# A cross-attention and mixture-of-experts kernel: filler matrix products on TensorE, another order of loads, logits one step later, one normalisation on VectorE

## The reference, cut to what matters

```python
def _L0_xattn_ref(q, k, v, igate_kernel, igate_bias, fgate_kernel, fgate_bias, outnorm_scale):
    x = concatenate([q, k, v], axis=-1)
    ig, fg = x @ igate_kernel + igate_bias, x @ fgate_kernel + fgate_bias
    # per head: log_D = (cs - cs^T, lower triangle) + ig^T, cs = cumsum(log_sigmoid(fg))
    # D = exp(log_D - max), C = (q k^T / sqrt(64)) * D
    # h = C / (max(|sum C|, exp(-max)) + 1e-6) @ v; then normalised per head, times scale
def _L0_ffn_ref(x, router_w, w1, w2):
    logits = einsum('nc,ec->ne', xf, router_w)          # 8 experts, two chosen
    h = gelu(einsum('nc,ech->enh', xf, w1)); y = einsum('enh,ehc->enc', h, w2)
    out = einsum('ne,enc->nc', comb, y)
x = x + _L0_xattn_ref(_layernorm(x), ctx, ctx, ...)     # x: (32, 128, 256) float32
x = x + _L0_ffn_ref(_layernorm(x), router_w, w1, w2)
```

## Time and profile before

| what | value |
|---|---|
| median of 3 runs (lowest to highest) | 759.17 us (758.35 to 761.41) |
| the profiled execution's own time | 766.17 us |
| its span | 764.3 us |
| TensorE busy in the span | 631.3 us (83%) |
| VectorE / ScalarE / GpSimd busy | 393.1 / 315.4 / 245.1 us |
| mean granted TensorE clock | 0.835 of 2.4 GHz |

### The profile page before, as it was taken

One profiled execution on the slowest core, in us unless ns is written; L12 is line 12 of the kernel. 1 busy time (PEld: TensorE's weight loads), 2 busy tenths in 40 slices (PEclk: granted clock), 3 DMA queues, 4 the chain that ended last, 5 costly groups with the idle time before them and its releaser, 6 DMA issues.

```text
span 764.3 us, 18354 instructions
## 1 busy us (share of the span) xinstructions
PE 631.3 (83%) x5879; PEld 504.2 (66%) x5879; DVE 393.1 (51%) x1094; ACT 315.4 (41%) x614; POOL 245.1 (32%) x192
## 2 busy tenths in 40 slices
PE   0684968779898994307999999999999999999991
PEld 0554756566877864206877777777777777777780
DVE  1452746667584555503555555555555555555550
ACT  1451562626444322102444444444444444444440
POOL 1101221626466266710222313233133231331322
PEclk9999856565565555557999999999999999999996
DMA  9878438294462122392385493943947639458321
GB/s 316 284 258 322 155 149 302 92 323 157 142 239 94 35 84 84 112 338 84 51 286 137 87 332 48 307 112 56 310 109 212 208 53 320 100 114 306 56 37 21
DMA packets 58964, 130.52 MB, mean 171 GB/s; under 512 B 6384, under 2 KB 38384, under 8 KB 57904
## 3 DMA queue, kind: packets, MB, share of 16 engines
q1 hardware_dynamic: 44384, 110.91, 40.8%
q0 software_dynamic: 13392, 18.10, 13.3%
q10 hardware_dynamic: 1152, 1.07, 0.4%
HBM read 188.49 MB, written 40.13 MB: 299 GB/s over the span
## 4 chain that ended last, share of the span: by engine, by line
PE 67%; DMA 12%; issue 6%; ACT 5%; DVE 4%; SPq 3%; POOL 2%; ACTq 1%; POOLq 0%; DVEq 0%
PE bank L661 15%; PE bank L647 9%; PE bank L649 9%; PE bank L648 8%; PE bank L663 8%; DMA xa<-in_x 7%; PE bank L540 4%; PE bank L565 3%; PE bank L483 3%; PE bank L525 2%; PE bank L510 2%; DMA out<-ct,dst 2%; PE bank L631 2%; POOL rows L1288 1%; DMA xrow<-rows 1%
## 5 line engine op out<-in xcount | busy, mean ns | idle before, releaser
L647 PE MATMUL bank<-dt,wring 128*128 128x128 f16 x1136 | 199.6, 220 | 2.4 <-ACT ct L824 1.2
L649 PE MATMUL bank<-dt,wring 128*128 128x128 f16 x1136 | 199.7, 220 | 0.0
L648 PE MATMUL bank<-dt,wring 128*128 128x128 f16 x1136 | 199.7, 220 | 0.0
L661 PE MATMUL bank<-wring,ct 128*128 128x512 f16 x568 | 192.5, 379 | 0.9 <-DVE ct L1222 0.7
L822 ACT ACTIVATE dt<-bank 128x512 f32<-128x512 f32 x142 | 84.9, 598 | 217.5 <-PE bank L649 211.0
L1222 DVE TENSOR_TENSOR ct<-dt,ct 128x512 f16<-128x512 f32 x142 | 98.4, 693 | 140.8 <-PE bank L663 99.2
L663 PE MATMUL bank<-wring,ct 128*128 128x256 f16 x568 | 154.8, 273 | 0.0
L1324 POOL DMA_INDIRECT out<-ct,dst x48 | 76.0, 1583 | 216.8 <-DMA out<-ct,dst 92.3
L647 PEld LDWEIGHTS bank<-dt,wring 128*128 128x128 f16 x1136 | 111.7, 98 | 27.0 <-issue 14.3
L648 PEld LDWEIGHTS bank<-dt,wring 128*128 128x128 f16 x1136 | 111.8, 98 | 0.9
L649 PEld LDWEIGHTS bank<-dt,wring 128*128 128x128 f16 x1136 | 111.9, 98 | 0.0
(11 more groups left out here) (140 smaller groups left out, 852.3 us busy)
## 6 DMA issues: line engine op xcount, KB each, us to landing
wring<-wsplit SPq DMA_DIRECT2D x284, 512.0 KB
wring<-in_w SPq DMA_DIRECT2D x16, 1024.0 KB, 11.4
xrow<-rows SPq DMA_DIRECT2D x71, 130.0 KB
wsplit<-wring SPq DMA_DIRECT2D x4, 2048.0 KB, 8.4
wsplit<-wcv SPq DMA_DIRECT2D x4, 2048.0 KB, 7.7
xa<-in_x SPq DMA_DIRECT2D x8, 512.0 KB, 10.7
kT<-in_ctx_t SPq DMA_DIRECT2D x8, 512.0 KB, 10.1
ctn<-in_ctx SPq DMA_DIRECT2D x8, 512.0 KB, 10.1
```

Source lines behind the costliest of these rows:

```text
L647: pe.matmul(o, hi, xT[k][:, c, :], start=(c == 0), stop=False)
L648: pe.matmul(o, hi, xT[k][:, CK + c, :], start=False, stop=False)
L649: mm = pe.matmul(o, lo, xT[k][:, c, :], start=False, stop=(c == CK - 1))
L661: pe.matmul(YP[k][:, 0:2 * D], gh[a][:, m4, :], wring[:, k, w:w + 2 * D], start=(a == 0 and m4 == 0), stop=False, skip_group_check=True)
```

## The change

- TensorE: a helper `dense` issues bfloat16 products of the identity with part of the mask into parts of accumulation banks whose contents nobody reads. Three of 256 columns follow each of the first three sequences of `gates`, two of 248 columns stand ahead of each `values`, and one of 256 columns follows each of the first three sequences of `logits`.
- TensorE: `logits` moves from the end of its step (for group m) to the next step (for group l), between `turn(n,0)` and `scores(t,0)`.
- SyncE: in a step the loads come first, and x is loaded one group further ahead (k + 1); then the weights that were split in the step before are stored, then the x1 of two steps back. At the start the loads of the first experts' weights come behind the constants and behind the keys and context of group 1.
- `SPLIT` gives each of the steps -1 to 6 one expert.
- The normalisation of x1 is done on VectorE, in the place of `x1_shift`, by one operation with two per-row scalars; ScalarE's `x1_norm` and the vector nm2 are gone.
- VectorE: the first operations of the router's chain come after `head_norm`.

```diff
-SPLIT = {-2: (0,), -1: (1, 2), 0: (3,), 1: (4,), 2: (5,), 3: (6,), 4: (7,)}
+SPLIT = {e - 1: (e,) for e in range(NE)}
...
             load_k(0)
+            sp.dma_start(gate_b[:, :, :], gate_b_in).then_inc(s_cst, 16)
             load_c(0)
-            sp.dma_start(gate_b[:, :, :], gate_b_in).then_inc(s_cst, 16)
             load_x(1)
-            load_w(0)
             sp.dma_start(cbf[:, :], cb.bitcast(BF16)).then_inc(s_cbf, 16)
...
             sp.dma_start(rwT[:, :, :], rw_t).then_inc(s_cst, 16)
+            load_k(1)
+            load_c(1)
+            load_w(0)
+            load_x(2)
...
-                if k is not None and k > 0:
-                    if k > 1:
-                        load_x(k)
+
+                if k is not None and k > 1:
                     load_k(k)
                     load_c(k)
-                for e in SPLIT.get(T, ()):
+                    if k + 1 < NG:
+                        load_x(k + 1)
+                for e in SPLIT.get(T - 1, ()):
                     store_w(e)
                     if e + 2 < NE:
                         load_w(e + 2)
-                if m is not None:
-                    store_x1(m)
+                if l is not None:
+                    store_x1(l)
...
+            def dense(o, count):
+
+                for _ in range(count):
+                    pe.matmul(o, cbf[:, B_IDENT:B_IDENT + P], cbf[:, B_MASK:B_MASK + o.shape[1]],
+                              start=True, stop=True, skip_group_check=True)
...
+                    if b < G - 1:
+                        dense(SB[:, 256:512], 3)
                 mm.then_inc(s_gt, 1)
...
+                dense(VB[b][:, 264:512], 2)
                 for h4 in range(NH):
...
+                    if b < G - 1:
+                        dense(SB[:, 256:512], 1)
                 mm.then_inc(s_lg, 1)
...
                 if n is not None:
                     turn(n, 0)
+                if l is not None:
+                    logits(l)
...
                     router_turn(m, 1)
-                    logits(m)
...
-                if m is not None:
-                    x1_norm(m)
...
-            def x1_shift(g):
+            def x1_norm(g):
                 dve.wait_ge(s_rs2, g + 1)
-                after(dve, s_xn2, 2 * g)
-                dve.scalar_tensor_tensor(nm2[:, :], mv2[:, :, 0], -1.0, rs2[:, :], ALU.mult, ALU.mult
-                                         ).then_inc(s_nm2, 1)
+                after(dve, s_sc[g % 2], 16 * (2 * G * (g // 2) + 1))
+                for b in range(G):
+                    ins = dve.tensor_scalar(rowb[g % 2][:, b, 0:D], xa[:, G * g + b, :], mv2[:, b, 0:1],
+                                            rs2[:, b:b + 1], ALU.subtract, ALU.mult)
+                    if b % 2 == 1:
+                        ins.then_inc(s_xn2, 1)
```

More of the change, by code:

```diff
@@ L159, in build @@
         rs2 = sb("rs2", [P, G])
-        nm2 = sb("nm2", [P, G])
         rT = sb("rT", [P, G, CK, P])
@@ L280, in build @@
         s_rs2 = sem("x1_rstd")
-        s_nm2 = sem("x1_shift")
         s_xn2 = sem("x1_normed")
@@ L458, in _ @@
             pe.wait_ge(s_gws, 1)
+            pe.wait_ge(s_cbf, 16)
+            def dense(o, count):
+                for _ in range(count):
+                    pe.matmul(o, cbf[:, B_IDENT:B_IDENT + P], cbf[:, B_MASK:B_MASK + o.shape[1]],
+                              start=True, stop=True, skip_group_check=True)
             def turn(g, h):
@@ L581, in step @@
                 if t is not None:
-                    if t == 0:
-                        pe.wait_ge(s_cbf, 16)
                     logd(t, 0)
@@ L747, in weights_high @@
                                ).then_inc(s_wh2, 1)
[L749 to L756, removed]
             def router_turned(g, h):
@@ L1090, in if_l @@
                         f(l, *a)
+                if_m(head_norm)
                 if_l(router, 0)
-                if_m(head_norm)
+                if_m(head_gamma)
                 if_l(router, 1)
-                if_m(head_gamma)
-                if_l(router, 2)
                 if t is not None:
                     scores(t, 0, 0)
+                if_l(router, 2)
+                if_m(residual)
                 if_l(router, 3)
-                if_m(residual)
                 if_l(router, 4)
@@ L1138, in step @@
                 if_l(slots)
-                if_m(x1_shift)
+                if_m(x1_norm)
                 if n is not None:
@@ L1263, in x1_rstd @@
                 after(pool, s_xn2, 2 * g)
-                after(pool, s_nm2, g)
                 pool.tensor_tensor(rs2[:, :], ve2[:, :], mhalf[:, 0:G], ALU.pow).then_inc(s_rs2, 1)
```

## The result

The change takes **737.84 us** (median of 4 runs, 732.68 to 741.41), beside 758.76 us for the kernel before on the same chip: a ratio of 0.972 (0.965 to 0.979). The forecast was 721 us in a range of 703 to 750: the sign and the range held, but 17 of the 38 us that were forecast are missing. The profiled execution took 736.62 us with a span of 734.8 us and a mean clock of 0.843.

The account below looks back on a forecast made before the run. Late x (steps 0 to 3) and TensorE, mostly at the lower clock level, bound the first part. Start 29.6, steps 28, 27.8, 145 and 24 make 254.4 against 293.3 us; draining +1; 38 off 759.2 gives 721 us, range 703 to 750.

Parts of the forecast that it names:

- the start: Before step 0: two megabytes of weights no longer ahead of x, gaining 6.6 us, so step 0 begins at 29.6 us.
- the loads: SyncE issues x a whole step earlier: -10.1 us in step 0, -4.9 us in each of steps 1 to 3.
- the clock's term: Full steps: fillers and moved logits raise TensorE's time at the upper clock level to 9.2 us, giving a 29.0 us step.
- F: TensorE's time at the upper clock level in a step; about 5 us before, forecast 9.2 us for a full step.
- plus 0.6 idle: TensorE in a full step: only 0.6 us idle added to 37.6 us of work at the lower clock level.
- the logits' wait: TensorE ahead of the logits: its wait for ScalarE goes when they move, -2.4 us in a full step.
- the router's chain on VectorE: Would start later with the moved logits; VectorE reaches it about in time, cost nothing; without that cover, up to 4 us.
- the x1 norm: On VectorE: four operations a step, 1.2 us in all, upper end 3.3; off the path unless VectorE is the bound.
- step 0, 1 and 7: Forecast lengths: step 0 28.0 us, step 1 27.8 us, step 7 24 us to the end of its head statistics.
- the draining: After the head statistics: draining gains six fillers, +1 us.
- the fillers pay where F grows: TensorE's full step: 20 fillers cost 4.8 us at the lower clock level and pay only if upper-level time grows.
- The rival of fillers without effect: Upper-level clock time stays 5 us, full steps take 33.2 us, gain 7.5 us: 752 us; chance 0.20.

Follow-up runs that it names:

- no_fill: The whole change with its filler products taken out; 728.04 us, 0.955 of the kernel before.
- loads_only: The kernel before with only SyncE's new load order and one expert for each step; 733.91 us, 0.963 of the kernel before.
- copy_first: The whole change with VectorE's copy of the logits ahead of head_norm, as before; 730.07 us, 0.956 of the kernel before.
- norm_scalar: The whole change with the x1 normalisation back on ScalarE, as before; 731.41 us, 0.961 of the kernel before.

## Why the prediction was right, and where it was wrong

**Right: the start and the loads, though not their size.** The start was forecast at 29.6 us and came at 29.9 (28.3 in no_fill), and no load of x is waited for in the steps. loads_only shows this term by itself, with the table of experts: 26 us. It was the only one that the gain needed. But what the prediction priced for it comes to 34.9 us: 6.6 at the start, 13.6 in step 0, and 4.9 in each of steps 1 to 3. Of the 9.8 us for steps 2 and 3 the trace of loads_only shows 0.6: the idle time went, and the clock was lower in the work that took its place.

**Right: the size of the clock's term, on the average.** I took F = 9.2 us at the upper level for a full step. From the windows the five steps have 10.3, 17.2, 10.4, 10.3 and 0 us: a mean of 9.6. TensorE's work of a full step was forecast at 37.6 us at the lower level; busy time plus F gives 38.0. What a mean hides is the scatter: step 6 stayed at 0.50 throughout and took 35.6 us, step 3 had 0.81 and took 27.7. The same kernel had 0.65 in one trace and 0.69 in another over steps 2 to 6. That the size came out is in part luck: the fillers brought only 2.1 to 4.4 us of it, and without them it was already 7.3 us a step, not the 5 that the sum started from.

**Wrong: "plus 0.6 idle".** This is the step that failed. I took the logits' wait off (2.4 us a step) and let nothing come for it; measured idle is 14.2 us in five steps, 2.8 each, as much as in steps 4 and 5 before (2.8 and 3.0 us; 0.6 in step 6, by the earlier trace rows). The missing 2.2 us a step is the whole difference between 29.0 and 31.2. The prediction did ask what would be late next, but it asked only for the router's chain on VectorE ("cost nothing; without that cover, up to 4 us"), and not who on TensorE waits for that chain's first operation: the gates, through the shared bank. copy_first shows that this wait, up to 1.4 us each time, is one of the causes. Nor did it ask what stands behind the x1 norm on VectorE: it priced the norm right (1.2 us forecast, 1.30 from its start to the scan's) and called it off the path, while the maximum's turn waits for the very next operation, for 4.5 us in five waits (0.6 in norm_scalar).

**Wrong: step 0, 1 and 7.** Step 0 took 19.6 us in this trace instead of 28.0. By its rows it ran at the lower level at first (the first `logd`'s products, 1.01 us at 29.89) and at the upper from 36.9 us on (the second's, 0.62 us), although the clock's column, which does not tell the levels apart this early, reads 1.00. In the second trace it took 26.75 us, so this is luck of the trace and not a gain that was missed. Steps 1 and 7 were 3.8 and 3.4 us over: in step 1 TensorE idles for 4.0 us of 31.6 (in the second trace for 0.9 of 28.7), in step 7 for 5.4 of 27.4. Step 7's term had no wait in it, and there is one of 4.5 us ahead of its second scores. By the rows it hangs on the last expert's low halves, which the new table lets run into this step, and on GpSimd's powers; loads_only has 2.3 us of it, and no run takes the two apart. Together with 11.2 us in steps 2 to 6 and 0.3 at the start this is the 10.3 us by which the head statistics came later than forecast; the draining gave 2 back.

**Wrong: that the fillers pay where F grows.** The prediction said so and took the growth as enough. Its own numbers held the break-even: 4.8 us a step go in, so F must grow from 5 to 9.8, and the F of 9.2 lay under that. The same sum without fillers, 32.8 + 0.6 - 5, is 28.4 us, less than the 29.0 with them; I never wrote it down. no_fill bears it out: 0.955 against 0.972 and 0.970, and 30.5 us as the mean of its steps 2 to 6 against 31.2 and 30.9. The rival of fillers without effect is refuted by the clock and by its 752 us; what holds of it is that the fillers gained nothing. As to the rule of the Trainium skill (TensorE: Matmul & The Clock Gate, Part 4) that transposes do not count as activity in the same way, the runs do not separate it: in the change the rises of steps 2 to 5 come behind the router's transposes and with `logd`, step 6 has the same order and no rise (0.50), and no run here took either out.

**The base.** Half of the 16.8 us between 721 and 737.84 is no step of the sum. The profile's own time fell by 29.6 us where 38 was forecast: 8.4 us. The other 8.2 us (the rest is rounding) come from the execution: that of before was 7.0 us over its median and that of after 1.2 us under. Its excess was not something that the change would carry along, and in the later comparisons the kernel before had medians of 760 to 763 us rather than 759.

## What to carry to other kernels

When a consumer is moved, list everything that the moved work's output holds up, a shared buffer among it: here the gates of the next step waited for a copy of 0.18 us behind 5.6 us of VectorE's other work. Filler products are to be judged by what they cost at each level of the clock against the time they gain, and their raising of the clock alone says nothing: here 37, 47 to 59 and 80 us at the upper level in the same five steps went with ratios of 0.955, 0.970 to 0.972 and 0.980. A single step of a single trace proves little where the clock moves: step 0 of one and the same kernel took 19.6 and 26.8 us. And where a change has many parts, run its plainest part alone; the order of the loads, with the table of experts, carried all of this one.

## What the runs showed of the hardware

Three fillers in the gates cost 0.32 us at the upper level and 0.59 at the lower, less than the 0.39 and 0.72 that were worked out from the 512-column products. The x1 norm, a one-input float32 operation of 128x256 between SBUF tensors with two per-row scalars, takes 408 ns on VectorE (median of 32, 386 to 416), as long as the statistics operation of the same shape (0.42 us):

```profile
L884 DVE TENSOR_SCALAR rowb<-xa,mv,rs x32: 386/408/416, 73.1 to 278.7; 128x256 f32<-128x256 f32 x32
```

The doubling that the Trainium skill (VectorE: DVE Perf Modes, on the mode 2×_2P) leads one to expect does not show in it; the measurement decides. The mask operation still takes 1.83 us where it meets GpSimd (L1013 in step 2), as it did before.
